# One range clear per stage, statistics beside loads or in a turn, weights loaded a stage early, and an aggregator that sums a whole step into four PSUM banks

## The reference

```
xn = layernorm(x)
x  = x + gnn0(xn, src, dst) + mix0(xn)        # 4 heads, softmax over each node's edges
x  = x + ffn0(layernorm(x))                   # 8 experts, the best 2 of them
xn = layernorm(x)
x  = x + gnn1(xn, src, dst) + mix1(xn)        # as gnn0, with another table; then a linear layer
x  = x + ffn1(layernorm(x))                   # 8 experts, all weighted

# the heart of gnn0 and gnn1, per head:
e     = leaky_relu(s[row] + d[col])
ex    = exp(e - segment_max(e, row))
den   = segment_sum(ex, row)
out   = segment_sum((ex / den[row]) * hW[col], row)
```

## Time and profile before

| | us |
|---|---|
| median of 3 runs | 7189.6 (7188.1 to 7196.35) |
| the profiled execution | 7195.71, its span 7193.5 |
| PE busy | 4905.2 (68%) |
| DVE busy | 4588.6 (64%) |
| POOL busy | 3420.2 (48%) |
| ACT busy | 1642.4 (23%) |
| PE's granted clock, mean | 0.837 |
| pass 1, first to last gather | 599.62 to 2697.26 |

### The profile page before, as it was taken

One profiled execution on the slowest core, in us unless ns is written; L12 is line 12 of the kernel. 1 busy time (PEld: TensorE's weight loads), 2 busy tenths in 40 slices (PEclk: granted clock), 3 DMA queues, 4 the chain that ended last, 5 costly groups with the idle time before them and its releaser, 6 DMA issues. The chain is left out here.

```text
span 7193.5 us, 103224 instructions
## 1 busy us (share of the span) xinstructions
PE 4905.2 (68%) x21356; PEld 3575.9 (50%) x21357; DVE 4588.6 (64%) x9157; ACT 1642.4 (23%) x4448; POOL 3420.2 (48%) x3713
## 2 busy tenths in 40 slices
PE   1236666676766762289666777766777655999999
PEld 0135555555555552256433444445555543666666
DVE  8976787887878777422356666667777756333333
ACT  5112323332322322012120000002222211333332
POOL 0005777777777770422107777777777740000000
PEclk8568888888988885599888888888888877899999
DMA  6013323222222252322345555555555561000001
GB/s 124 0 27 74 57 56 57 57 57 57 58 57 56 57 50 39 129 62 64 95 143 138 139 139 139 139 140 147 148 147 147 148 107 38 0 9 4 9 4 36
DMA packets 422045, 566.81 MB, mean 79 GB/s; under 512 B 135161, under 2 KB 278034, under 8 KB 421830
## 3 DMA queue, kind: packets, MB, share of 16 engines
q0 software_dynamic: 143392, 306.68, 20.0%
q1 hardware_dynamic: 278566, 259.13, 13.3%
HBM read 487.78 MB, written 77.74 MB: 79 GB/s over the span
## 5 line engine op out<-in xcount | busy, mean ns | idle before, releaser
L544 POOL DMA_INDIRECT got<-table,st_idx x3328 | 3169.4, 952 | 1106.3 <-issue 1009.3
L616 PE MATMUL ps_sum<-weighted,hot 128*128 128x260 f32 x6656 | 1838.9, 434 | 173.9 <-DVE acc L690 169.7
L616 PEld LDWEIGHTS ps_sum<-weighted,hot 128*128 128x128 f32 x6656 | 1405.0, 221 | 547.0 <-DVE acc L690 235.5
L690 DVE TENSOR_TENSOR acc<-acc,ps_sum 128x260 f32 x1664 | 707.2, 425 | 682.4 <-PE ps_sum L616 534.2
L603 PE MATMUL ps_score<-score_split,hot_t 128*128 x3328 | 249.1, 185 | 1153.6 <-DVE z L670 1124.1
L682 DVE TENSOR_TENSOR weighted<-got,ps_weight 128x2048 f32<-128x2048 f32 x416 | 949.0, 2281 | 5.1 <-ACT weighted L578 0.8
L603 PEld LDWEIGHTS ps_score<-score_split,hot_t 128*128 128x128 bf16 x3328 | 194.8, 101 | 1336.9 <-issue 1321.8
L575 ACT ACTIVATE ps_weight<-z 128x32 f32<-128x32 f32 x416 | 83.6, 201 | 2773.0 <-DVE z L670 2773.0
L2797 DVE SCALAR_TENSOR_TENSOR x_res<-ps_yf,comb,x_res 128x256 f32 x392 | 189.6, 484 | 641.4 <-PE ps_yf L2706 641.4
L641 DVE TENSOR_TENSOR hot<-ps_score,row_loc 128x1024 f32<-128x1024 f32 x416 | 506.9, 1218 | 7.2 <-issue 0.2
L659 DVE TENSOR_REDUCE row_score<-ps_score 128x64 f32<-128x192 f32 (+1 forms) x416 | 167.5, 403 | 356.2 <-DMA got<-table,st_idx 355.9
(11 more groups left out here) (459 smaller groups left out, 7147.9 us busy)
## 6 DMA issues: line engine op xcount, KB each, us to landing
spread<-row_list SPq DMA_DIRECT2D x416, 256.0 KB
got<-table,st_idx POOLq DMA_INDIRECT x3328
xin_e<-slots_in SPq DMA_DIRECT2D x108, 128.5 KB, 2.0
slots_in<-nought SPq DMA_DIRECT2D x1, 13824.0 KB
gate_xin<-ball_rows SPq DMA_DIRECT2D x99, 128.0 KB
got_y<-y_rows SPq DMA_DIRECT2D x12, 896.0 KB, 7.4
table<-row SPq DMA_DIRECT2D x50, 130.0 KB, 2.1
ball_rows<-xt SPq DMA_DIRECT2D x10, 640.0 KB, 5.6
```

The lines of the kernel that those rows point to most:

```text
L544: pool.indirect_dma_start(got[:, r, k, :], None, table, bass.IndirectOffsetOnAxis(ap=st_idx[:, r, k:k + 1], axis=0))\
L616: last = nc.tensor.matmul(ps_g[:, p % 2, 0:AW], hot[:, r % 2, k, :], weighted[:, r % 2, k, :], start=(k == 2 * p), stop=(k == 2 * p + 1))
L690: nc.vector.tensor_tensor(acc[:, ds(b * AW, AW)], acc[:, ds(b * AW, AW)], ps_g[:, p % 2, 0:AW], ALU.add).then_inc(added, 1)
```

## The change

- `semaphore` and `stage`: inside a stage the handles are kept in a list and cleared together at its end, before the barrier.
- `stage_ln_stats` becomes a class `LnStats`. Statistics 1 are taken inside `load_wide`, with the loads issued in the same block; statistics 3 inside `fill_folded`; statistics 4 inside turn 3, tile by tile behind the add into x, and their chain at that stage's end.
- `fill_l1` becomes `TableWeights`: `load` is issued on SP at the end of `stage_collect`, `blank` is a memset on POOL there, and `fold` runs in the L1 tables' stage. A stage named `early` lies around all stages from turn 1 to the L1 peaks and holds the two semaphores.
- The aggregator: `ps_sum` has four banks in place of two, so a whole step is summed at once, and its sums are added one step later. ACT weighs two steps ahead, DVE scales first, then makes the transposed one-hot, the exponents, the four adds of the step before, the one-hot, and the guest's two parts. `GateMix` has three banks in place of four, with two new waits for its projection.

```diff
 def semaphore(nc, name):
     handle = nc.alloc_semaphore(name)
-    yield handle
-    nc.clear_and_free_semaphores([handle])
+    if held:
+        held[-1].append(handle)
+        yield handle
+    else:
+        yield handle
+        nc.clear_and_free_semaphores([handle])
...
     with ExitStack() as own:
         own.callback(nc.all_engine_barrier)
+        def clear_all():
+            nc.clear_and_free_semaphores(held.pop())
+        held.append([])
+        own.callback(clear_all)
         yield own
...
-        ps_g = own.enter_context(nc.psum_tensor("ps_sum" + tag, [P, 2, 512], F32))
-        ps_w = own.enter_context(nc.psum_tensor("ps_weight" + tag, [P, 512], F32))
+        ps_g = own.enter_context(nc.psum_tensor("ps_sum" + tag, [P, KP, 512], F32))
...
+        high, peak, weights = (ps_s[:, BEHIND + k * KT * 4:BEHIND + (k + 1) * KT * 4].rearrange("p (k c) -> p k c", c=4) for k in range(3))
+        count_to = ps_g[:, KP - 1, AW:AW + P]
...
                 if not (first and r < 2):
-                    act.wait_ge(summed, (i - 1) * KP)
+                    act.wait_ge(summed, i - 1)
...
                 pe.wait_ge(hot_t_ready, i + 1)
                 if not (first and r == 0):
-                    pe.wait_ge(z_ready, i)
+                    pe.wait_ge(w_ready, i * 2 - 1)
...
-            def sum_up(turn, r, first, half):
+            def sum_up(turn, r, first, last_turn):
                 i = turn * STEP_RING + r
                 pe.wait_ge(hot_ready, i + 1)
                 pe.wait_ge(scaled, i + 1)
-                for p in half:
-                    if not (first and r == 0 and p < 2):
-                        pe.wait_ge(added, i * KP + (p - 1))
+                for p in range(KP):
+                    if not (first and r == 0):
+                        pe.wait_ge(added, i * KP + (p + 1 - KP))
+                    if p == KP - 1 and exists(last_turn, r, 1):
+                        pe.wait_ge(hot_ready, i + 2)
...
             def one_turn(turn, first, last):
                 for r in range(STEP_RING):
-                    sum_up(turn, r, first, range(KP // 2))
                     if exists(last, r, 2):
                         t, q = later(turn, r, 2)
                         score(t, q, first and r + 2 < STEP_RING)
+                    sum_up(turn, r, first, last)
                     guest.tensor(pe, turn, r)
-                    sum_up(turn, r, first, range(KP // 2, KP))
...
-            def scale(turn, r):
+            def scale(turn, r, last):
                 i = turn * STEP_RING + r
                 dve.wait_ge(w_ready, i * 2 + 2)
+                if exists(last, r, 1):
+                    dve.wait_ge(scored, i + 2)
...
+                    scale(turn, r, last)
+                    if summed_before:
+                        blocks = blocks_of(i * KP - KP, KP, DVE)
                     if exists(last, r, 2):
                         one_hot_t(*later(turn, r, 2))
                     if exists(last, r, 1):
                         exponents(*later(turn, r, 1))
-                    add(turn, r, first, LOW, blocks[len(HIGH):])
+                    if summed_before:
+                        add(t, q, first and r == 1, blocks)
+                    if exists(last, r, 1):
+                        one_hot(*later(turn, r, 1), first and r + 1 < STEP_RING)
+                    guest.vector_first(dve, turn, r)
                     guest.vector_then(dve, turn, r)
...
+class LnStats:
+    def tile(self, i):
+        self.nc.vector.bn_stats(self.stats[:, ds(i * 6, 6)], self.source(i)).then_inc(self.got, 1)
...
-                        nc.vector.scalar_tensor_tensor(xr, row[:, r, :], 0.0, xr, ALU.max, ALU.add)
+                        nc.vector.scalar_tensor_tensor(xr, row[:, r, :], 0.0, xr, ALU.max, ALU.add).then_inc(x_new, 1)
+                        if next_norm is not None and not (first and r == 0):
+                            dve.wait_ge(x_new, i)
+                            stats.tile(i - 1)
...
                 both(HALF2 - 1, False, last=True)
+                if next_norm is not None:
+                    dve.wait_ge(x_new, NTP)
+                    stats.tile(NTP - 1)
+                    dve.wait_ge(xs_ready, NTP)
+                    stats.finish(dve)
...
         @block.vector
         def _(dve):
+            if stats is not None:
+                stats.vector(dve)
             if bias is not None:
...
                 for s in range(2, SUPS):
                     load(s)
+                weights.load(sp)
+
+            @block.gpsimd
+            def _(pool):
+                weights.blank()
...
-        self.banks = own.enter_context(nc.psum_tensor("ps_gate_mix", [P, 4, 512], F32))
+        self.banks = own.enter_context(nc.psum_tensor("ps_gate_mix", [P, 3, 512], F32))
...
-            stage_ln_stats(nc, g, "_1")
...
-                stage_ln_stats(nc, g, "_3", source=new_row)
...
-            stage_ln_stats(nc, g, "_4")
```

More of the change, by code:

```diff
@@ L583, in one_turn @@
                         stage_idx(turn + 1, r)
-                    if exists(last, r, 1):
-                        t, q = later(turn, r, 1)
-                        weigh(t, q, first and r + 1 < STEP_RING)
+                    if exists(last, r, 2):
+                        t, q = later(turn, r, 2)
+                        weigh(t, q, first and r + 2 < STEP_RING)
                     guest.scalar(act, turn, r)
@@ L682, in scale, with add @@
                 nc.vector.tensor_tensor(out, v, w, ALU.mult).then_inc(scaled, 1)
-            def add(turn, r, first, half, blocks):
+            def add(turn, r, first, blocks):
                 i = turn * STEP_RING + r
-                for p, b in zip(half, blocks):
-                    dve.wait_ge(summed, i * KP + p + 1)
-                    if not (first and r == 0 and p == 0):
+                dve.wait_ge(summed, i + 1)
+                for p, b in enumerate(blocks):
+                    if not (first and p == 0):
                         dve.wait_ge(added, i * KP + p)
-                    nc.vector.tensor_tensor(acc[:, ds(b * AW, AW)], acc[:, ds(b * AW, AW)], ps_g[:, p % 2, 0:AW],
+                    nc.vector.tensor_tensor(acc[:, ds(b * AW, AW)], acc[:, ds(b * AW, AW)], ps_g[:, p, 0:AW],
                                             ALU.add).then_inc(added, 1)
-            LOW, HIGH = range(KP // 2), range(KP // 2, KP)
             DVE = mybir.EngineType.DVE
@@ L698, in one_turn @@
                     t, q = (turn, r - 1) if r else (turn - 1, STEP_RING - 1)
[L699 to L704, removed]
-                        add(t, q, first, HIGH, blocks[:len(HIGH)])
-                    guest.vector_first(dve, turn, r)
-                    if exists(last, r, 1):
-                        one_hot(*later(turn, r, 1), first and r + 1 < STEP_RING)
+                    summed_before = not (first and r == 0)
+                    scale(turn, r, last)
+                    if summed_before:
+                        blocks = blocks_of(i * KP - KP, KP, DVE)
                     if exists(last, r, 2):
@@ L2056, in _ @@
+        made, biased, wide = (own.enter_context(semaphore(nc, name)) for name in ("a1_made", "b1_made", "bet_spread"))
+        with nc.Block() as block:
             @block.tensor
             def _(pe):
-                pe.wait_ge(loaded, 16 * 14)
                 for c in range(2):
@@ L2139, in pb @@
             return own.enter_context(nc.psum_tensor(name, shape, F32))
-        wl = sb("wl_2", [P, 2, W])
-        bias = sb("bias_bc_2", [P, W])
-        fill(own, wl, bias)
+        wl, bias = weights.wl, weights.bias
+        weights.fold(own)
         xs = sb("xs_2", [P, XS, D])
@@ L2491, in tensor @@
             for c in range(2):
-                last = nc.tensor.matmul(bank[:, 3, 0:D], self.ogt[:, c, :], mix.wqt[:, c, :], start=(c == 0), stop=(c == 1))
+                last = nc.tensor.matmul(bank[:, 0, D:2 * D], self.ogt[:, c, :], mix.wqt[:, c, :], start=(c == 0), stop=(c == 1))
             last.then_inc(self.proj, 1)
```

237 lines of the change are left out of this document (132 added, 105 removed).

## The result

The changed kernel takes 7143.1 us (median of 4 runs, 7142.1 to 7144.78) where the kernel before takes 7188.9 (4 runs beside it): 45.8 us less, a ratio of 0.9937 (95% interval 0.9924 to 0.995). In a later set of runs it gave 0.9935 (0.9921 to 0.9948). The prediction was 7133 with 7100 to 7172. The direction, the range and most of the terms held; two terms did not, and a third was not in the sum.

A forecast was written before the change was run, and what follows sets the result against it. POOL's gathers were taken to bound the aggregator's two passes, and whatever ends last each stage outside them. Terms summed to -56.0 us, taken off the 7189.6 median for 7133, range 7100 to 7172.

The forecast's parts named there:

- The clears: Stage ends: clearing semaphores together saves 249 clears at 0.147 us each, -36.6 us.
- Rival (c): Stage ends: a range clear costs by width or the drain waits as long, 0 to -19 instead of -36.6; chance 0.07.
- Statistics 1 and 3: Starts of turns 1 and 3: loads issued beside the statistics remove DVE's waits, -4.8 and -6.2 us.
- Statistics 4: Between turns 3 and 4: 16.9 us of stage go, about 5 come back in turn 3's loop, -12 us.
- Weights: Start of the L1 tables: loads issued at collect's end remove the wait for 14 loads, -9.1 us.
- The aggregator's tail: End of each aggregator pass: the last step's adds follow the whole step, +5.9 us a pass, +11.8 together.
- The aggregator's steady state: Aggregator passes: POOL keeps its own gather pitch, nothing is gained, and DVE's 36.2 us a turn fits within 40.3.
- rival (d): Aggregator passes: DVE's new order moves POOL's gather pitch, shifting the sum by 20 us either way; chance 0.06.
- Rival (a): Turn 4: shorter PE idle before it keeps the full clock, an estimated -25 us, so 7108; chance 0.07.
- Rival (b): Aggregator pass 1: new PE-DVE ping-pong makes DVE's turn pass POOL's 40.3 us, giving 7258; chance 0.08.

The follow-up runs named there:

- the last experiment: Changed kernel with the aggregator of before, the guest's denominators in PSUM and the transposed one-hot's lane number read from PSUM, against the kernel before: 7131.2 us, 0.9913.

## Why the prediction was right, and where it was wrong

- **The clears:** -36.6 predicted, -37.3 measured alone (there the three statistics stages still stand, whose clears the prediction counted apart; by the same pitch that would be 1.3 more). Rival (c) fell, though a range does cost a little by its width.
- **Statistics 1 and 3:** -4.8 and -6.2, measured -4.4 (turn 1 whole) and -6.3 (reciprocal to first normalised tile 9.7 us, then 3.4). Right.
- **Statistics 4:** -12. Taking the edit out gave 12.4: 17.0 for the stage, as said, and 4.5 for the statistics in the loop, where I had 5. The term was right. Against the kernel before the loop grew by 8.0, 3.5 of them by something else in the new code.
- **Weights:** -9.1. The wait of 9.23 went and the last y was 0.3 later, but the L1 tables as a whole gained 8.3 and collect lost 2.8. Of the latter 2.4 lie ahead of the last y load: DVE's first wait for y rows is 9.4 us instead of 7.5. Collect varies from 81.8 to 84.9 between programs, so this much is not a finding. The 1.4 us more in the tables are PE's clock: its granted level rose 7 us after the first tile here and 4 before.
- **The aggregator's tail:** +5.9 a pass was mis-sized, it is +3.3 and +3.0. The structure was right: PE starts both last steps only when the last gather has landed, since the adds that it waits for stand behind DVE's exponents. But the two sixteens took 5.43 and 3.75 us: the last 16 matmuls ran at the full clock, where I had priced both at the 6.01 of a row at the lower one. From the last row score to the last add are 13.7 us against 10.4. Timeline of the end of pass 1 and a window in it:

```profile
2719.08 0.36 DVE L670 TENSOR_REDUCE row_score<-ps_score 128x64 f32<-128x192 f32 x1 [6.87 <-DMA got<-table,st_idx]
2719.99 2.13 DVE L703 TENSOR_TENSOR acc<-acc,ps_sum 128x260 f32 x4
2720.56 5.43 PE L630 MATMUL ps_sum<-weighted,hot 128*128 128x260 f32 x16 [6.07 <-DVE acc L703]
2726.72 3.75 PE L630 MATMUL ps_sum<-weighted,hot 128*128 128x260 f32 x16 [0.72 <-DVE acc L703]
```

```profile
2724.20:2731.00 6.80, 5.54 (x25) 4.17 (x23) 3.33 (x6) 0.00 (x0) 0.00 (x0) 1.00 0.01 2
```

- **The aggregator's steady state:** "nothing is gained, and it fits" was right of DVE and PE and wrong of POOL. This is the step that failed: I held POOL's pitch to be its own. It rose from 1.2608 to 1.2661 and from 1.2532 to 1.2568 us, +8.8 and +6.1 from first gather to last, by more stretched gathers (80 to 120, 31 to 54). The 6.1 by itself is hardly more than the 5.8 by which two profiles of the kernel before differ; on one chip, two profiles with either aggregator, the rise is 9 in pass 1 and 7 in pass 2. That the operands and the place decide is shown by the runs above that moved them. That the new order puts more gathers in the bad place can be counted: in pass 2 those lengthened behind a one-hot begun 0.1 to 0.4 us earlier rose from 26 (42 in the second profile of the kernel before) to 85 (91). Which of the moved instructions does it was not tried. It was my rival (d), at 0.06, and it came beside the forecast instead of in its place. In this pair of profiles less than the tails' surplus and this together shows in the end (+11.8 predicted, +16.1 measured), since the last gather landed 2.6 and 2.7 us sooner after its issue. That is not the change's doing: the kernel before has lags of 28.0 and 24.4 us in its own two profiles. On one chip, with lags of 27.4 to 27.5 us in pass 1 with either aggregator, the two passes cost 12.8 and 8.7 us, 21.5 where I had 11.8.
- **Turn 4:** -5.8 us that no term had and no run explains.
- **The base:** profile against profile the sum was -56.0 and the measured difference -53.2, 2.8 apart. The other 7 of the 10 us between 7133 and 7143 come of taking the sum off a median that lay 6.1 under its profile. That the sum came so close is partly luck: turn 4's gain hides more than the 4.3 us by which the aggregator's term fell short in this pair.

Rival (a), the clock in turn 4, did not come: 10 idle us let it fall as 28 had. Rival (b) did not come either: in the changed kernel POOL waited for neither PE nor DVE in the stretches shown. It came in the last experiment, by another cause.

The Trainium skill (SBUF — State Buffer, box "The DVE blocks DMA trap") bears on this more than I gave it: it has GpSimd kept from writing descriptors while DVE holds the shared port, and the same page ("Who interferes with whom") adds instructions with two SBUF inputs against GpSimd operations that read SBUF. The trace agrees that the gather waits for DVE's instruction to end (0.81 to 0.82 us from there to the gather's own end, in all 63 and all 38 counted above), and that a product with two SBUF inputs does it; in which mode the one-hot ran the trace does not show. The page also infers that a `tensor_tensor` (what each of the guest's two products is) does not stop the writing of descriptors; here 38 of 38 gathers issued by POOL were lengthened by one, and the measurement decides. A gather lost 0.03 to 0.5 us, what was left of DVE's instruction, and one that began elsewhere lost nothing.

## What to carry to other kernels

Where POOL's indirect DMAs set the pace, read DVE's instructions beside the long ones: an operand moved from SBUF to PSUM gave 10.7 us where a rebuilt aggregator had cost 16 to 24, and the order of DVE's work inside a step moved a pass by 25. Taking waits from an engine that has slack gained nothing here, and the new order slowed the engine that it follows. Count the lengthened instructions by where they begin, not only how many pass a threshold, and take a second profile of the same kernel before reading a few us into one stage. A semaphore cleared one at a time was 0.147 us on every engine's path; a range for the stage took 0.04 to 0.26 us.

## What the hardware showed that I had not expected

- A gather issued just after DVE starts an instruction of these two kinds is longer itself (1.18 or 1.31 us instead of 0.95), with the gap ahead of it unchanged at 0.30, and it ends 0.81 to 0.82 us after DVE's instruction does, wherever in that window it began.
- The last row score, which waits for the last gather, comes 24 to 30 us after that gather's issue in every kernel; passes that issue later did not all land later by as much (pass 1, from last issue to last row score: 28.0 before, 25.4 in the changed kernel, and 24.4 in the second profile of the kernel before, so it is not the change's).
